# Causal attention: scores taken twice, with the exponentials made key by key and not turned

## The reference, cut to what matters

```python
q = (x @ Wq + bq).reshape(b, s, 16, 64)
k = (x @ Wk + bk).reshape(b, s, 4, 64)
v = (x @ Wv + bv).reshape(b, s, 4, 64)
q, k = _rotary(q), _rotary(k)             # t * cos + rotated halves * sin
qg = q.reshape(b, s, 4, 4, 64)
logits = jnp.einsum('bqhgd,bkhd->bhgqk', qg, k) / sqrt(64)
logits = jnp.where(causal, logits, -1e30)
w = jax.nn.softmax(logits, axis=-1)
out = jnp.einsum('bhgqk,bkhd->bqhgd', w, v).reshape(b, s, 1024)
x = _layernorm(x + out @ Wo + bo)
```

## Time and profile before

| | us |
|---|---|
| Time before, median of 3 runs (lowest, highest) | 1377.93 (1376.24, 1378.32) |
| Span of the profiled execution | 1376.4 |
| Attention stage in it | 350 to about 973 |

### The profile page before, as it was taken

How to read it: one execution, slowest core, us unless ns; L and a number is a source line. 1 busy time by engine, 2 the same in 40 slices (tenths; PEclk the granted TensorE clock), 3 DMA queues, 4 the chain that set the end, 5 groups by cost and what they waited for, 6 DMA issues and landing times. The chain is left out here.

```text
span 1376.4 us, 24979 instructions
## 1 busy us (share of the span) xinstructions
PE 1186.4 (86%) x8059; PEld 868.3 (63%) x8060; DVE 865.8 (63%) x1528; ACT 763.2 (55%) x2082; POOL 586.3 (43%) x616
## 2 busy tenths in 40 slices
PE   7888589676899999999999999999898439999991
PEld 4544367455566767777666777776676337888881
DVE  2588799874345545665355555675688666777773
ACT  2498447434555656666455565664366245565652
POOL 1155447656445331431553322200267415666663
PEclk9999789888699999999999999999999658999996
DMA  9100000001010010000100000100730232232325
GB/s 300 40 1 1 0 1 2 1 16 31 17 32 16 16 26 10 14 16 6 42 16 17 16 17 1 47 2 1 269 99 1 74 122 43 46 52 47 50 46 138
DMA packets 42136, 58.27 MB, mean 42 GB/s; under 512 B 6608, under 2 KB 34640, under 8 KB 42032
## 3 DMA queue, kind: packets, MB, share of 16 engines
q1 hardware_dynamic: 34544, 46.70, 11.3%
q0 software_dynamic: 7488, 10.23, 4.6%
HBM read 32.80 MB, written 13.63 MB: 34 GB/s over the span
## 5 line engine op out<-in xcount | busy, mean ns | idle before, releaser
L2016 DVE TENSOR_REDUCE ga_neg_top<-ps 128x1 f32<-128x128 f32 (+7 forms) x256 | 182.0, 753 | 195.2 <-PE ps L1786 194.8
L1897 ACT ACTIVATE ga_e<-ps,ga_neg_top 128x128 f32<-128x128 f32 (+7 forms) x256 | 188.4, 744 | 7.6 <-DVE ga_neg_top L2016 6.8
L1906 ACT COPY ga_e_tr<-ps 128x512 f32<-128x512 f32 (+3 forms) x192 | 92.2, 480 | 174.4 <-PE ps L1795 171.7
L1795 PE MATMUL ps<-ident,ga_e 128*128 128x128 f32 x1152 | 165.1, 278 | 0.9 <-DVE ga_e_tr L2024 0.8
L1811 PE MATMUL ps<-ga_e_tr,ga_v 128*64 128x256 f32 x1152 | 151.7, 391 | 4.1 <-ACT ga_att L1914 4.1
L1795 PEld LDWEIGHTS ps<-ident,ga_e 128*128 128x128 f32 x1152 | 123.3, 142 | 28.0 <-ACT ga_e L1897 14.7
L2024 DVE COPY ga_e_tr<-ps 128x128 f32<-128x128 f32 (+3 forms) x192 | 105.9, 552 | 35.1 <-PE ps L1795 34.8
L1971 POOL TENSOR_TENSOR ga_q_lo<-shared,ga_q_hi 128x1024 fp32r<-128x1024 f32 x15 | 35.6, 2370 | 176.1 <-ACT ga_q_hi L1887 176.1
L2566 DVE TENSOR_TENSOR ex_w_lo<-ex_gate_up,ex_w_hi 128x1024 fp32r<-128x1024 f32 x78 | 92.4, 1226 | 26.6 <-ACT ex_w_hi L2426 26.4
L1811 PEld LDWEIGHTS ps<-ga_e_tr,ga_v 128*64 128x64 f32 x1152 | 72.5, 136 | 49.0 <-issue 23.4
L2426 ACT CAST ex_w_hi<-ex_gate_up 128x1024 fp32r x78 | 77.9, 1046 | 23.7 <-issue 16.4
(11 more groups left out here) (330 smaller groups left out, 2721.4 us busy)
## 6 DMA issues: line engine op xcount, KB each, us to landing
shared<-shared SPq DMA_DIRECT2D x80, 128.0 KB, 2.3
ex_gate_up<-in_ex_gate_up SPq DMA_DIRECT2D x1, 8192.0 KB, 24.3
ex_down<-in_ex_down SPq DMA_DIRECT2D x1, 4096.0 KB, 35.7
x_tr<-in_x_tr SPq DMA_DIRECT2D x4, 512.0 KB, 7.0
x_nat<-in_x SPq DMA_DIRECT2D x1, 2048.0 KB, 11.7
gated_rows<-shared SPq DMA_DIRECT2D x8, 256.0 KB, 2.2
gated_rows<-x_tr SPq DMA_DIRECT2D x8, 256.0 KB, 2.3
x_tr<-summed_rows SPq DMA_DIRECT2D x8, 256.0 KB, 5.1
```

What stands on the lines that cost most here:

```text
L1795: last = nc.tensor.transpose(ps_tr[n % 2][:, (kb - k0) * P:(kb - k0 + 1) * P], e[half][t % 2][:, kb * P:(kb + 1) * P], core.ident[:])
L1897: nc.scalar.activation(e[half][t % 2][:, 0:blocks(t) * P], ps_scores(t, half), ACT.Exp, bias=neg_top[t % 2][:, half:half + 1], accum_out=s ...
L1906: nc.scalar.copy(e_tr[g % 2][:, k0:k1, half, t % 2 * P:(t % 2 + 1) * P], ps_tr[n % 2][:, 0:(k1 - k0) * P].rearrange("p (k t) -> p k t", t= ...
L2016: nc.vector.tensor_reduce(neg_top[t % 2][:, half:half + 1], ps_scores(t, half), AX.X, ALU.max, negate=True).then_inc(top_ready, 1)
```

## The change

The work of a tile is laid out in two parts.

*Row maxima.* `top_scores` makes only the hi x hi product with queries as rows, in "units" of up to 512 columns for each half (L1787 of the changed kernel), masks it (L1792), and VectorE reduces it (L2061) to the negative maxima; for tiles of more than four blocks two partial ones are merged (L2066). This runs one to two tiles ahead, from ten ticks before the first tile. PSUM banks 0 and 1 hold one unit at a time. At i = 6 of tile J the maxima of tile J + 1 are turned in `ps_piece` (L1800), and ScalarE writes four scaled copies of them (`spread_shift`).

*Keys as rows.* A step (J, c, kb) is one key block for one pair of key heads and all four ticks of it: 144 steps, each 128 keys by 512 columns for each half. `key_scores` first writes the negative maxima by a product (L1819), then adds the three products (L1823), and on the diagonal a mask of 512 columns (L1827). ScalarE makes one exponential over 128x1024 with no bias and no sum. The result is already turned: `weigh_values` (L1840) multiplies it with the values. The sums over keys come from `add_keys` (L2007): VectorE adds half 0 of the blocks, GpSimd half 1, 112 additions of 128x512 each; then `sum_keys` multiplies the added block with a matrix of ones (L1855) into `ps_piece`, VectorE inverts it (L2071, 128x512 from PSUM) and multiplies (L2075). That happens twice per tile, for c = 0 at i = 6 and for c = 1 at i = 1 of the next tile.

Queries are now projected three tiles ahead and rotated two ahead (three buffers); GpSimd's three rotations stand in three ticks (i = 0, 1, 2), with additions between them. Four buffers of exponentials replace the others.

```diff
-    STEPS = range(PAIR_COUNT + 9)
+    AHEAD, DRAIN = 10, 9
+    TICKS = range(-AHEAD, TICK_COUNT + DRAIN)
+    Q_BUFFERS, E_BUFFERS = 3, 4
+    steps = [(J, c, kb) for J in range(TILES) for c in range(KV_PAIRS) for kb in range(blocks(J))]
+        place = (s - first_step[J]) * QT // (KV_PAIRS * blocks(J))
+        steps_at.setdefault(J * QT + place, []).append(s)
...
+        n_rows = max(1, PIECE // blocks(J))
+        own = [(J, c, r, r + n_rows, n) for c in range(KV_PAIRS) for r in range(0, R, n_rows) for n in range((blocks(J) - 1) // PIECE + 1)]
+            place = (J - 2) * QT + 6 + i * QT // len(own)
...
+    def top_turn_at(t):
+        return J + 1 if i == 6 and 0 <= J + 1 < TILES else None
+    def sums_at(t):
+        if i == 6 and 0 <= J < TILES:
+            return J * KV_PAIRS
+        if i == 1 and 1 <= J <= TILES:
+            return (J - 1) * KV_PAIRS + 1
...
+                def top_scores(u):
+                    need(pe, top_ready, u)
+                    for r in range(r0, r1):
+                        for half in range(2):
+                            last = nc.tensor.matmul(ps_top[:, half, columns], q_hi[J % Q_BUFFERS][rows, c * R + r, :],
+                                                    k_hi[k_slot(b, n)][rows, c, 0:width], start=(r == r0), stop=(r == r1 - 1 and not diagonal))
...
+                def turn_top(J):
+                    take_piece_bank((shift_ready, J + 1))
+                    nc.tensor.transpose(ps_piece[:, 0:P], neg_top[J % 2][:].rearrange("p h x -> p (h x)"), core.ident[:]).then_inc(top_turned, 1)
+                def key_scores(s):
+                    need(pe, e_ready, s - 1)
+                        last = nc.tensor.matmul(out(half), pair_rows[rows, c, :], shift[J % 2][rows, :, :], start=True, stop=False)
+                    for i, (ks, qs) in enumerate(((k_hi, q_hi), (k_hi, q_lo), (k_lo, q_hi))):
...
-                def transpose_chunk(t, i):
...
-                def spread_recip(J, part):
...
+                def sum_keys(g):
+                    take_piece_bank((recip_ready, g + 1))
+                        pe.wait_ge(add_ready, adds_through[s])
+                        pe.wait_ge(pool_add_ready, adds_through[s])
+                        last = nc.tensor.matmul(ps_piece[half * HD:(half + 1) * HD, :], ones[:], of_keys[:, half, :], start=True, stop=True)
...
+            def add_keys(engine, ops, ready, half, s):
+                engine.wait_ge(e_ready, s + 1)
+                ops.tensor_tensor(added[g % 2][:, half, :], before[:, half, :], e[s % E_BUFFERS][:, half, :], ALU.add).then_inc(ready, 1)
...
+                def normalise(g):
+                    dve.wait_ge(sums_ready, g + 1)
+                    nc.vector.reciprocal(recip[:], ps_piece).then_inc(recip_ready, 1)
+                    nc.vector.tensor_tensor(values, values, recip[:], ALU.mult).then_inc(att_done, 1)
```

More of the change, by code:

```diff
@@ L1624, in k_slot, with group, ends_group @@
+    def group(s):
+        return steps[s][0] * KV_PAIRS + steps[s][1]
+    def ends_group(s):
+        J, c, kb = steps[s]
+        return kb == blocks(J) - 1
+    adds_through = [sum(kb >= 1 for _, _, kb in steps[:s + 1]) for s in range(len(steps))]
+    tops_merged = [sum(blocks(i) > PIECE for i in range(J + 1)) for J in range(TILES)]
     def k_slot(b, n):
@@ new lines, in split_high_q, with spread_shift @@
+                    nc.scalar.copy(q_hi[J % Q_BUFFERS][:].rearrange("p g t -> p (g t)"), q_raw[:]).then_inc(q_hi_ready, 1)
+                def spread_shift(J):
+                    act.wait_ge(top_turned, J + 1)
+                    if J >= 2:
+                        act.wait_ge(s_ready, first_step[J - 1])
+                    for r in range(R):
+                        last = nc.scalar.activation(shift[J % 2][:, r, :], ps_piece[:, 0:P], ACT.Copy, scale=top_rows[:, KV_PAIRS + r:KV_PAIRS + r + 1])
+                    last.then_inc(shift_ready, 1)
```

502 lines of the change are left out of this document (247 added, 255 removed).

## The result

The changed kernel takes 1592.07 us (median of 4 runs, 1588.65 to 1600.78), the kernel before, beside it, 1378.12. The ratio is 1.157, interval 1.154 to 1.160: 214 us slower. The direction of the forecast (1480, 102 us slower) is right; the size is twice what was forecast, and the time lies above the range that ended at 1545.

What follows compares the result with a forecast made beforehand. TensorE was taken to bound the attention stage. Work -53 us, waits +157 and 3 less for lost idle time gave +101 on the 1376.4 us span, 1477.4, stated as 1480 us; range 1415 to 1545.

Steps and rivals of the forecast that it cites:

- the clock: Rival: after 26 waits of TensorE at i=2 and i=6 the granted clock drops, 1.7 us each, 44 us; 1525 us, chance 0.15.
- TensorE's work: Attention stage: turns and spreading gone (-173 us), scores +75, masks +15, sums +32, turned maxima +3, value products -5; sum -53 us.
- The idle time: TensorE's waits in the attention stage: 157 us added, less 3 us of earlier idle time lost in the last ticks.
- Three of the signs: Expected in the changed profile: TensorE's stage busy time down about 50 us, clock 1.00 outside waits, tile 11 at 45 to 50 us.
- (a): At i=6 TensorE waits for the PSUM bank: scaled copies 1.5 us, wide reciprocal 3.6 us; 66, 4 and 7 us.
- The slower reciprocal: Rival: the wide reciprocal takes 4.4 us instead of 3.35, adding 29 us; 1510 us, chance 0.05.
- (b): At i=2 VectorE's reciprocal, multiply, addition and maximum in one row make TensorE wait: 13 x 3.0 = 39 us.
- (c): Two row-maximum units one step apart: the second waits until VectorE has read the first; 28 x 0.5 = 14 us.
- (d): The sum at i=1 waits for GpSimd's last addition, behind a rotation; 1.5 to 4 us late in about six tiles, 12 us.
- (e): First tile: maxima must be found, turned and spread before the first exponential, and queries prepared; 15 us, 5 to 30.
- The streaming inversion: Rival: the wide reciprocal streams at 0.69 us, shrinking waits behind it; +28 us, 1406 us, chance 0.06.
- the faster kernel: Rival: streaming reciprocal, other waits covered by queued work, first tiles prepared beside the stage before; -33 us, 1345 us, chance 0.08.

## Why the prediction was wrong in size

Two steps of the prediction failed: the sum had nothing for the clock, which cost 70 us, and TensorE's work was to fall by 53 us and fell by 14. The idle time came out right as a whole, and that in part by luck.

**The bound and the kind of loss** were read rightly: TensorE loses its gain by waiting in order behind single buffers. Three of the signs that the prediction named came otherwise: TensorE's busy time in the stage rose by 56 us where it was to fall by 50, the clock is not 1.00 outside the waits, and tile 11 takes 55 us (907 to 962), not 45 to 50.

**(a) The inversion and the bank.** Forecast 3.35 us each and waits of 1.5 and 3.6 at i = 6. Tile 11:

```profile
944.94 0.28 PE L1800 MATMUL ps<-ident,ga_neg_top 128*128 128x128 f32 x1
946.45 1.59 PE L1855 MATMUL ps<-ga_added,ga_ones 128*64 128x512 f32 x4 [1.23 <-ACT ga_shift L1920]
951.49 3.78 PE L1249 MATMUL ps<-x_tr,wide_weights 128*128 128x128 f32 x16 [3.45 <-DVE ga_recip L2071]
```

The waits are 1.23 and 3.45. All of (a) was put at 77 us; before projections and behind ScalarE's scaled copies the trace has 45.0 + 10.4 + 20.2 = 76. That the slope of the two small inversions held over a factor of 16 made this term. The slower reciprocal did not come.
**(b), (c) Maxima.** Forecast 53 us, measured 65 (the part of the 71.6 that VectorE's maxima ended). Behind an inversion the units waited 11 times, 2.4 to 5.7 us and 4.1 on average, where 13 waits of 3.0 stood. The two with no slowed multiply or addition in VectorE's row waited 2.8 and 2.4 us, those with both slowed 3.4 to 5.7: the excess goes with the meetings at SBUF, which stood in the range and not in the sum.

**(d), (e).** GpSimd's late additions: 12 forecast, 18.6 measured, 5.2 of it at the very end of the stage. The start was put at 15 beyond (a): up to 394 us TensorE is idle 16.9 us, of which 6.4 are waits of the kinds in (a), so 10.5 are left. The idle term as a whole, 154 against 158, is closer than its parts. The new waits come to 176 us where 157 stood; of the 20 us of waits that the kernel before had, 18 are gone, where only 3 were taken off. The two errors nearly cancel, and that is luck.

**Work: the first term that was mis-sized**, -53 for -14. By the spacing of starts, with stretches at half clock left out or halved: the maximum products are 384 of 0.16 us (61), and I gave them a third of the old products (38). In the timeline of tile 12 above, a pair of them that stands alone between other work takes 0.33 (973.36 to 973.69), a pair in the middle of a group of like products 0.23 (972.67 to 972.90). The old products, on the other side, had cost 131 and not 115, so the growth was 86 where 75 stood (+11). Value products got no cheaper but dearer, 148 from 142, where I had taken 5 off: +11. The old form's masks came to 23 from 16 beside the wide ones at 17 (+9). The turns had cost 144, not 150 (+6). The sums, the turns of the maxima and the output projection make some 3 more. Together that is about 40, of which each part is good to 1 or 2 us: the distance from -53 to -14.

**Clock: the second, and the larger one.** I carried it as a rival with 26 losses of 1.7 us, 44 us, and gave it 0.15. But the forecast's own idle term is made of waits like those after which the clock falls in the earlier trace rows, so it belonged in the sum. Its size was too small as well: 30 stretches with 2.6 us lost in each, 78 us, because TensorE stays at 1.2 GHz for 7.3 us on average, often with a second wait inside. The two stretches in the earlier trace rows are among the shortest of the trace before. It also has longer ones, such as this, in which TensorE comes out of a wait of 5.59 us:

```profile
324.90:331.70 6.80, 4.55 (x22) 4.55 (x23) 1.40 (x4) 2.41 (x6) 6.35 (x8) 0.50 0.01 2
...
327.15 0.69 PE L1500 MATMUL ps<-ident,x_nat 128*128 128x128 f32 x2 [5.59 <-ACT x_nat L1459]
```

With 44 in the sum the forecast would have been 1524, still 68 us short; with 70 and the work right, 1589.

**The rivals.** The streaming inversion and the faster kernel, which rests on it, are excluded by the 3357 ns alone. The kernel with the inversion left out has the price that the streaming rival spoke of, and takes 1490, not 1406: again the work (+43) and the clock (+40).
